# A similarity mixer on Trainium2: which engine takes the relus and which the squares

## The reference, cut to what matters

```
xn = xf * rsqrt(max(sum(xf * xf), 1e-12))      # per position, 64 channels
sim = einsum('bic,bjc->bij', xn, xn)           # 3136 x 3136 per image
sim = power(relu(sim), 2)
y = einsum('bij,bjc->bic', sim, x @ W)
```

## Time and profile before

| what | value |
|---|---|
| median of 3 runs | 5306.62 us (5291.68 to 5308.91) |
| span of the profiled execution | 5295.0 us (no time of its own is listed beside it) |
| busy: TensorE, VectorE, ScalarE, GpSimd | 4009.5, 3288.8, 2502.0, 2389.5 us |
| mean granted TensorE clock | 0.859 of full |
| instructions of L937 (relu), L955 and L471 (squares) | 896, 336 and 560 |

### The profile page before, as it was taken

The page is one execution under the profiler, slowest core; times in us unless marked ns, Lnnn a source line. Parts: engine busy times, 40 slices in busy tenths (PEclk is TensorE's granted clock), DMA queues, the critical chain, the costliest instruction groups (busy, mean ns, idle before and its releaser), DMA issues.

```text
span 5295.0 us, 75229 instructions
## 1 busy us (share of the span) xinstructions
PE 4009.5 (76%) x23964; PEld 2039.4 (39%) x23964; DVE 3288.8 (62%) x4487; ACT 2502.0 (47%) x4177; POOL 2389.5 (45%) x2694
## 2 busy tenths in 40 slices
PE   6887896879788896879788796879778796883222
PEld 2333343344334343344334443344334443342112
DVE  5356556666667666666567666676666665664554
ACT  5645553456445564455544564455544564450001
POOL 0000772427452673427543573517643473416780
PEclk9988897989899897989899897989899897995555
DMA  2001221122111321122211321122211221124261
GB/s 60 7 0 25 65 68 39 55 61 67 50 55 40 85 66 43 53 60 68 57 47 39 84 66 46 58 56 70 61 47 39 78 67 41 49 58 97 75 148 39
DMA packets 351180, 303.37 MB, mean 57 GB/s; under 512 B 281424, under 2 KB 285888, under 8 KB 350944
## 3 DMA queue, kind: packets, MB, share of 16 engines
q0 software_dynamic: 96768, 231.34, 14.9%
q1 hardware_dynamic: 254176, 68.98, 6.2%
HBM read 252.58 MB, written 47.60 MB: 57 GB/s over the span
## 4 chain that ended last, share of the span: by engine, by line
PE 34%; POOL 26%; issue 16%; DVE 12%; another core or an unknown queue 4%; DVEq 3%; ACT 3%; DMA 1%; POOLq 0%; ACTq 0%; SPq 0%
PE PS L1114 30%; POOL G L334 25%; PE PS L1262 3%; DVE work L572 1%; DVE small L568 1%; POOL pool_cell L321 1%; ACT work L994 1%; DVE st L351 1%; PE PS L1153 1%; DVE G L382 1%; DVE small L515 1%; DVE tmp L419 1%; DMA G<-corner_table,index_now 1%; DVE xm L404 1%
## 5 line engine op out<-in xcount | busy, mean ns | idle before, releaser
L334 POOL DMA_INDIRECT G<-corner_table,index_now x2016 | 2264.6, 1123 | 621.4 <-issue 603.2
L321 POOL TENSOR_TENSOR pool_cell<-pool_cell 112x1 f32<-112x1 f32 x448 | 95.5, 213 | 2110.2 <-DVE value L388 937.4
L937 ACT ACTIVATE work<-PS 112x784 f32<-112x784 f32 x896 | 727.7, 822 | 660.1 <-DVE work L471 462.5
L382 DVE TENSOR_TENSOR G<-G,corner_w 112x768 f32<-112x768 f32 x672 | 636.0, 955 | 482.4 <-DMA G<-corner_table,index_now 481.6
L994 ACT ACTIVATE work<-PS,descale 128x448 f32<-128x448 f32 x896 | 566.6, 633 | 662.8 <-PE PS L1114 561.0
L572 DVE SCALAR_TENSOR_TENSOR work<-PS,descale,work 128x448 f32<-128x448 f32 x896 | 599.5, 682 | 450.8 <-ACT work L994 293.6
L1114 PE MATMUL PS<-work,xj 112*64 112x392 f32 x3584 | 818.3, 529 | 62.3 <-DVE work L471 50.4
L471 DVE TENSOR_TENSOR work<-work 112x784 f32<-112x784 f32 x560 | 545.2, 974 | 447.4 <-PE PS L1114 379.1
L1114 PE MATMUL PS<-xn_hl,xn_hh 128*112 128x392 f16 x1792 | 650.8, 363 | 66.8 <-issue 31.7
L1114 PE MATMUL PS<-xn_hl,xn_ll 128*112 128x392 f16 x1792 | 612.8, 342 | 0.0
L1114 PE MATMUL PS<-work,w3s 128*64 128x448 f32 x1792 | 463.3, 596 | 71.5 <-DVE small L568 59.1
(11 more groups left out here) (234 smaller groups left out, 5386.6 us busy)
## 6 DMA issues: line engine op xcount, KB each, us to landing
G<-corner_table,index_now POOLq DMA_INDIRECT x2016
corner_table<-xln SPq DMA_DIRECT2D x64, 392.0 KB
xin<-x SPq DMA_DIRECT2D x8, 784.0 KB
yw_scratch<-yw SPq DMA_DIRECT2D x8, 784.0 KB, 9.5
x_scratch<-xB SPq DMA_DIRECT2D x7, 784.0 KB, 7.9
corner_table<-G SPq DMA_DIRECT2D x4, 841.0 KB, 6.0
x<-x_scratch SPq DMA_DIRECT2D x4, 784.0 KB
split<-yw_scratch SPq DMA_DIRECT2D x4, 784.0 KB
```

What stands on the lines that cost most here:

```text
L334: GP.indirect_dma_start(G[0:TP, q, tap * 4 * C:(tap + 1) * 4 * C], None, table, bass.IndirectOffsetOnAxis(ap=index_now[:, q, tap:tap + 1], ...
L382: V.tensor_tensor(g, g, bc(w, 2, C), ALU.mult)
L937: A.activation(relu[:, u % 2], PS[u % 2][0:TP, :, 0:IW], ACT.Relu).then_inc(s["relu_done"], 1)
```

## The change

VectorE takes the relus of steps 1, 2, 4, 5 and 7 straight from PSUM as `max(x, 0)`, ScalarE those of steps 0, 3 and 6. ScalarE makes all eight squares, in place. The two slots of `relu` and the two of `sq` become one ring `sim` of four slots in the same memory; a slot is free for step `u` when `mix` of `u - 4` is done. TensorE waits for the relu of `u` on the semaphore of the engine that makes it, and for the square on `sq_done`. Piece 3 of a weighed tile moves from step 5 to step 6 in `MIX`.

```diff
-ACT_STEPS = (0, 3, 6)
+ACT_RELUS = (0, 3, 6)
-MIX = dict(sample=(0, 2, 4, 6), evac=(1, 3, 5), add=7, weigh=(0, 1, 3, 5, 7))
+MIX = dict(sample=(0, 2, 4, 6), evac=(1, 3, 5), add=7, weigh=(0, 1, 3, 6, 7))
+    SIMS = 4
-        relu = work[0:TP, 0:4 * IW].rearrange("p (q b n) -> p q b n", q=2, b=2)
-        sq = work[0:TP, 4 * IW:8 * IW].rearrange("p (q b n) -> p q b n", q=2, b=2)
+        sim = work[0:TP, 0:SIMS * 2 * IW].rearrange("p (q b n) -> p q b n", q=SIMS, b=2)
+        def relus(body_no, u):
+            if u in ACT_RELUS:
+                return s["relu_act"], body_no * ACT_N + ACT_RELUS.index(u) + 1
+            return s["relu_dve"], body_no * DVE_N + DVE_RELUS.index(u) + 1
+        def slot_mixed(half_no, g, u, first):
+            return 2 * half_no + g + u + 1 - SIMS + (0 if first and u < SIMS else 2)
 VectorE, mixer_body:
-                    if u in DVE_STEPS:
-                        dve.wait_ge(s["relu_done"], g + u + 1)
-                        dve.wait_ge(s["mixed"], 2 * half_no + g + u + 1)
-                        V.tensor_tensor(sq[:, u % 2], relu[:, u % 2], relu[:, u % 2], ALU.mult).then_inc(s["sq_dve"], 1)
+                    if u in DVE_RELUS:
+                        dve.wait_ge(s["sim_done"], g + u + 1)
+                        free = slot_mixed(half_no, g, u, first)
+                        if not (isinstance(free, int) and free <= 0):
+                            dve.wait_ge(s["mixed"], free)
+                        V.tensor_scalar(sim[:, u % SIMS], PS[u % 2][0:TP, :, 0:IW], 0.0, None, ALU.max).then_inc(s["relu_dve"], 1)
 ScalarE, mixer_body:
-                    if u + 1 < SPB or not last:
-                        ... wait for the square of u - 1
-                        relu_step(g + u + 1, u + 1)
-                    if u in ACT_STEPS:
-                        act.wait_ge(s["relu_done"], g + u + 1)
-                        act.wait_ge(s["mixed"], 2 * half_no + g + u + 1)
-                        A.activation(sq[:, u % 2], relu[:, u % 2], ACT.Square).then_inc(s["sq_act"], 1)
+                    if u + 1 in ACT_RELUS:
+                        relu_step(g, u + 1, half_no, first)
+                    if u == SPB - 1 and not last:
+                        relu_step(g + SPB, 0, half_no, False)
+                    done, count = relus(body_no, u)
+                    act.wait_ge(done, count)
+                    A.activation(sim[:, u % SIMS], sim[:, u % SIMS], ACT.Square).then_inc(s["sq_done"], 1)
 TensorE, mix and mixer_body:
-                if u in ACT_STEPS: ... wait on sq_act, else on sq_dve
+                pe.wait_ge(s["sq_done"], body_no * SPB + u + 1)
-                        pe.wait_ge(s["relu_done"], g + u + 1)
+                        pe.wait_ge(*relus(body_no, u))
                         sims(j0 + (u + 2) // 2, i0, u)
```

More of the change, by code:

```diff
@@ L54, in metaformer_kernel @@
     NW = 6
-    ACT_N = len(ACT_STEPS)
-    DVE_STEPS = tuple(u for u in range(SPB) if u not in ACT_STEPS)
-    DVE_N = len(DVE_STEPS)
+    ACT_N = len(ACT_RELUS)
+    DVE_RELUS = tuple(u for u in range(SPB) if u not in ACT_RELUS)
+    DVE_N = len(DVE_RELUS)
+    SIMS = 4
     table = nc.dram_tensor("corner_table", [SIDE * SIDE, 4 * C], f32).ap()
@@ L176, in metaformer_kernel @@
             x_loaded x1_added centered squared var_done std_done scaled h_cast split_done tr_done tr_cm
-            sim_done relu_done sq_act sq_dve mixed xj_ready z_ready y_done
+            sim_done relu_act relu_dve sq_done mixed xj_ready z_ready y_done
             logits_done sm_shift sm_exp disp_split disp_tr disp_cm
@@ L462, in mixer_norm, with mixer_body @@
                 split_l(n, None)
-            def mixer_body(g, half_no, tile, nxt, own=None):
+            def mixer_body(g, half_no, first, tile, nxt, own=None):
                 plan = MIX_FIRST if own else MIX
                 for u in range(SPB):
-                    if u in DVE_STEPS:
-                        dve.wait_ge(s["relu_done"], g + u + 1)
-                        dve.wait_ge(s["mixed"], 2 * half_no + g + u + 1)
-                        V.tensor_tensor(sq[:, u % 2], relu[:, u % 2], relu[:, u % 2], ALU.mult).then_inc(s["sq_dve"], 1)
+                    if u in DVE_RELUS:
[4 more added lines that the diff above has]
+                        V.tensor_scalar(sim[:, u % SIMS], PS[u % 2][0:TP, :, 0:IW], 0.0, None, ALU.max).then_inc(s["relu_dve"], 1)
                     for piece in range(5):
@@ L490, in body @@
                         first = back and half == 0 and isinstance(j, int) and j == 0
-                        mixer_body(g0 + j * SPB, k * 2 + half, (k - 1, j + t0) if back else None, nxt,
+                        mixer_body(g0 + j * SPB, k * 2 + half, isinstance(j, int) and j == 0,
+                                   (k - 1, j + t0) if back else None, nxt,
                                    (k - 1, 0, 0, 0) if first else None)
@@ L933, in stage_sources, with relu_step @@
                              xm[:, :, :].rearrange("p t c -> p (t c)")[:, bass.ds(j0 * C, JB * C)], ACT.Copy).then_inc(s["xj_ready"], 1)
-            def relu_step(s_no, u):
-                act.wait_ge(s["sim_done"], s_no + 1)
-                A.activation(relu[:, u % 2], PS[u % 2][0:TP, :, 0:IW], ACT.Relu).then_inc(s["relu_done"], 1)
+            def relu_step(g, u, half_no, first):
+                act.wait_ge(s["sim_done"], g + u + 1)
+                free = slot_mixed(half_no, g, u, first)
+                if not (isinstance(free, int) and free <= 0):
+                    act.wait_ge(s["mixed"], free)
+                A.activation(sim[:, u % SIMS], PS[u % 2][0:TP, :, 0:IW], ACT.Relu).then_inc(s["relu_act"], 1)
             def mixer_body(g, body_no, half_no, tile, first, last, next_sources, plan):
                 for u in range(SPB):
-                    if u + 1 < SPB or not last:
[L944 to L950, removed]
-                        relu_step(g + u + 1, u + 1)
-                    if u in ACT_STEPS:
-                        act.wait_ge(s["relu_done"], g + u + 1)
-                        act.wait_ge(s["mixed"], 2 * half_no + g + u + 1)
-                        A.activation(sq[:, u % 2], relu[:, u % 2], ACT.Square).then_inc(s["sq_act"], 1)
+                    if u + 1 in ACT_RELUS:
[5 more added lines that the diff above has]
+                    A.activation(sim[:, u % SIMS], sim[:, u % SIMS], ACT.Square).then_inc(s["sq_done"], 1)
                     for stage in range(3):
@@ L1232, in mixer @@
                     if not half:
-                        pe.wait_ge(s["relu_done"], g0 + SPH)
+                        pe.wait_ge(*relus(hn * BPH + BPH - 1, SPB - 2))
+                        pe.wait_ge(*relus(hn * BPH + BPH - 1, SPB - 1))
                         sims(0, i0 + 4 * IW, 0)
```

8 lines of the change are left out of this document (2 added, 6 removed).

## The result

The changed kernel takes 5521.27 us (median of 4 runs, 5501.08 to 5552.7) against 5305.34 for the one before: a ratio of 1.0407, 95% interval 1.0382 to 1.0431. The profiled execution has a span of 5498.9 us, 203.9 more than before. I had forecast 5298 and a range up to 5345.

The account below looks back on a forecast made before the run. TensorE and GpSimd's gathers were taken to bound the mixer closely. Per gathered image +1.5 - 2.1 - 0.6 = -1.2 us, seven of them -8.4, first image -0.6, together -9: 5298 us, range 5256 to 5345.

Parts of the forecast that it names:

- What bounds the kernel: Mixer: TensorE needs 14.09 us of a 14.87 us body; the 0.78 us of waiting, in step 2, laid to GpSimd's gathers.
- (1): Work per body: ScalarE +0.14 us, covered by TensorE (16 us without cover); VectorE's relu from PSUM 0.97, its load unchanged.
- (2): GpSimd's gathers per body: stretch from VectorE's two-SBUF-input products falls from 3.33 to 1.95 us, period to 13.5, no longer the bound.
- (3): Steady mixer bodies: relus queue behind VectorE's multiplications, `value` comes earlier; body from 14.87 to about 14.25 us, 0.62 saved.
- (4): First two bodies of each gathered mixer: step 3 later by 3.4 to 5.8 us; half 0 taken as +1.5.
- (5): Second half of each gathered mixer: four bodies save 2.1 us; the last body's stall of 5.28 us stays, 0.
- (6): Ends of halves: last relu and square on two engines, ready 0.3 us sooner, 16 times; -0.6 us per gathered image.
- Rival (b): Relus queued behind gather waits, stretch 2.55, bodies again 14.85, dearer ramp: +52 us, 5359; chance 0.23.
- (c): Relu from PSUM stretches gathers as a product does, GpSimd freed of nothing: body 15.6 us, +90, 5397; chance 0.05.

Follow-up runs that it names:

- e12: Kernel before with only the four-slot ring and squares in place, all relus on ScalarE, five squares on VectorE: 5212.67 us, ratio 0.9834.
- e15: The changed kernel with the fourth weighing piece back at step 5, where the kernel before takes 4985.21 us: 4954.34 us, ratio 0.9941.
- e10: Kernel before, its five VectorE products taking one input from PSUM (a minimum, so no squares): 5345.92 us, ratio 1.0085.
- e5: Kernel before, unchanged, run again for its trace: 5308.52 us, ratio 1.0009.
- e6: The changed kernel, unaltered, run again where the kernel before takes 5302.15 us: 5539.51 us, ratio 1.0435.
- e8: The changed kernel plus a tiny GpSimd addition after the second, fourth, sixth and eighth gather of each tile: 5263.63 us, ratio 0.9914.
- e18: The changed kernel with the fourth weighing piece back at step 5, where the kernel before takes 5376.62 us: 5693.59 us, ratio 1.0593.

## Why the prediction was wrong

The steps, by the traces of the change:

- What bounds the kernel: right about which engines, wrong about the cure. The waiting 0.78 us of a body lies in steps 2 and 3 (2.63 - 2.09 and 1.86 - 1.61), not in step 2 alone, and I laid it to GpSimd's period. e12, with the same engines at the same work and only more slots, loses most of it.
- (1) Work: right. 0.972 us for the relu; ScalarE has 10.9 us more, forecast 16.
- (2) GpSimd: the relief came as forecast. The mean gather fell from 1.123 to 1.035, and in front of L331, which starts a tile, GpSimd waits 1282.8 us for `value` (the kernel before: 937.4). In the body of e15 shown below the nine gathers from 1190.44 take 10.41 us, 1.16 in the mean and 2.04 of stretch in all, where I had walked to 1.15 and 1.95. The rule that I had read from a few gathers holds. By the Trainium skill, SBUF — State Buffer, "Who interferes with whom", a two-input product holds up no descriptor generation, which the section marks as inferred; with one product input moved to PSUM the gathers of e10 take 1.090 in the mean against 1.121 in e5 on the same chip, which speaks against it.
- (3) Bodies of 14.25: near where signals are in time, wrong where they are not. Over ten bodies of each of seven images (leaving out an image's first two and the last of each half) the mean is 14.80 in the kernel before, 16.68 in the change, 17.09 in e6 and 14.43 in e15. From e15's third image, the first matmul of a body's first step and of its step 2, and VectorE's first multiplication:

```profile
1190.60 0.37 PE L1123 MATMUL PS<-xn_hl,xn_hh 128*112 128x392 f16 x1
...
1190.77 0.96 DVE L392 TENSOR_TENSOR G<-G,corner_w 112x768 f32<-112x768 f32 x1 [1.32 <-DMA G<-corner_table,index_now]
...
1194.51 0.37 PE L1123 MATMUL PS<-xn_hl,xn_hh 128*112 128x392 f16 x1 [0.17 <-DVE work L483]
```

  The next body starts at 1204.99, so this one takes 14.39; the wait before the multiplication is 1.32 us (I had said 1.2), and step 2 is held 0.2 by the relu before it. In the first trace of the change three bodies in a row take 17.5, 15.2 and 16.5 (1335.62 to 1353.14, to 1368.38, to 1384.85), and steps 0 to 4 of them are unhindered: the stall sits in 5, 6 and 7, which no step of mine names.
- (4) Ramp: right in size. Step 3 of the second body comes 48.0 us after the image's first gather (1216.60 - 1168.62), 48.4 on the quick chip of e15; I had said 48 to 50.
- (5), (6) The half ends became the worst place, 21.6 us between steps (1299.17 to 1320.74) instead of 11.2 (1272.57 to 1283.80); I had forecast a small gain.

The step that failed is the use made of (2) in (3): I counted free gathers as a gain and asked only what their stretch cost GpSimd. What back-to-back gathers do to the others' signals had no term, and the wait for a signal I priced at 0.05 us. In the changed kernel 198 of 699 signals are over 0.3 us late instead, the mixers wait 407 us for signals after 2 before, and the body that was to fall from 14.87 to 14.25 takes 16.68 in the mean. Where that term is zero, the version with the piece at 5 comes to 0.994, near my forecast of 0.998. That nearness is no proof of the sum, since no trace of the kernel before on a quick chip shows its terms. Where the term isn't zero, the change costs 4 to 6%. Rival (b) had the right sign, with 5359, for a reason that e8 and e18 don't bear out, and even (c) stopped at 5397. The sum of (c) is also wrong in itself: two bodies that lose 1.5 us each make 3.0, not 1.5, which gives about 5407; the forecast doesn't use it.

The hint was in the rows that I had chosen myself. In the earlier trace rows L568 shows "remote 53.0", more than half of its idle time, and in the same view L999 and L925 had 242 more. All of it lies outside the mixers, where gathers are stretched least. I passed over it because the mixers had none (2 us of all remote waits). The products that I proposed to take away helped to keep it so, as e10 shows with 169 us once they no longer stretch the gathers.

## What to carry to other kernels

An idle time that the profile gives to a remote or unknown releaser in a kernel on one core is a cost to be explained before anything is moved. Ask what runs beside it, and whether the stage to be changed is spared only because something slows that down. And a change of several parts is worth taking apart: here the four-slot ring alone gave 1.7%, and the exchange of engines beside it turned that into a loss of 4 to 6% on every chip where the change ran unaltered, all of them slower ones.

## What the runs showed of the hardware

- TensorE's semaphore updates can come up to several us late (5.78 at most in the first trace of the change) while GpSimd issues indirect transfers; the matmuls themselves go on by the records. In time, they come 0.01 to 0.02 us after the matmul's end (e15). The other engines' updates in the mixers and among the experts are never late. The transfers keep pace: in a body of the first trace (1336 to 1349) the packets of each gather are done some 2.3 to 2.8 us after its start.
- It depends on the chip: none late of 784 in each of eight runs on two chips, 26 to 33% of the recorded ones in the changed kernel on four occasions elsewhere. The kernel before takes 4985 us on one chip and 5377 on another. That late signals make this difference fits the 374 us of remote waits in e5, but no run shows that the chips differ in nothing else.
- Where updates are late, some 11 to 19% of TensorE's similarity updates are missing from the trace (699 of 784 are there in the first trace of the change, 633 in e10). Updates of ScalarE and VectorE are missing there too. Each timed run was recorded as well, so whether the recording itself takes part in the delay, and a kernel that isn't recorded would lose less, wasn't tried; neither was what the signals and the transfers share. Both stay open.
